# First layer's cross attention (a1) and the gated stage behind it (p2) put into one block

## The reference

```python
x = _attn(_ln(x, g1, b1), _ln(x, g1, b1), Wq1, Wk1, Wv1, Wo1, bo1) + x
x = _attn(_ln(x, g2, b2), context, Wq2, Wk2, Wv2, Wo2, bo2) + x      # 16 heads of 64; scores, softmax, values
x = _geglu_ff(_ln(x, g3, b3), Wp, bp, Wf, bf) + x                    # a * gelu(gate) @ Wf; Wp is 256 x 2048, Wf 1024 x 256
# second layer: 16 heads of 16; self attention, gelu feed-forward, cross attention, gelu feed-forward
```

## Time and profile before

| | |
|---|---|
| median of 3 runs | 3474.93 us (3468.88 to 3476.86) |
| the profiled execution | 3473.62 us, span 3471.8 us |
| PE busy | 3212.7 us, 93% of the span |
| DVE, ACT, POOL busy | 2257.0, 1823.9, 1085.5 us |
| mean granted clock of PE | 0.952 |
| a1 on PE | 966.9 to 1999.4 us |
| p2 on PE | 2016.9 to about 2290 us |

### The profile page before, as it was taken

The page is one execution under the profiler, slowest core; times in us unless marked ns, Lnnn a source line. Parts: engine busy times, 40 slices in busy tenths (PEclk is TensorE's granted clock), DMA queues, the critical chain, the costliest instruction groups (busy, mean ns, idle before and its releaser), DMA issues. The chain is left out here.

```text
span 3471.8 us, 48148 instructions
## 1 busy us (share of the span) xinstructions
PE 3212.7 (93%) x17084; PEld 1842.8 (53%) x17084; DVE 2257.0 (65%) x4098; ACT 1823.9 (53%) x3369; POOL 1085.5 (31%) x537
## 2 busy tenths in 40 slices
PE   7969996999979999999999959979999699999989
PEld 5734443788744444444444447743477544444347
DVE  5447774444356666766666435569866499999844
ACT  4424444444424444444444424448766268888864
POOL 1036663000047777787777800002200000000000
PEclk9979998999979999999999979979999789999999
DMA  6888874999885666666766153154554723333140
GB/s 231 306 202 225 216 210 175 369 334 346 288 185 136 142 153 156 145 141 146 160 147 142 50 192 138 46 181 129 171 197 151 269 67 108 92 99 111 58 137 31
DMA packets 367126, 588.79 MB, mean 170 GB/s; under 512 B 47152, under 2 KB 197216, under 8 KB 365736
## 3 DMA queue, kind: packets, MB, share of 16 engines
q1 hardware_dynamic: 361710, 582.41, 56.8%
q10 hardware_dynamic: 5178, 3.31, 0.4%
HBM read 344.19 MB, written 241.29 MB: 169 GB/s over the span
## 5 line engine op out<-in xcount | busy, mean ns | idle before, releaser
L2164 ACT ACTIVATE a_prob<-a_ring 128x512 f32<-128x512 f32 (+1 forms) x1088 | 575.3, 602 | 665.7 <-PE a_ring L2069 588.9
L2190 DVE TENSOR_REDUCE a_blk_max<-a_ring 128x1 f32<-128x402 f32 x1024 | 519.4, 567 | 325.6 <-PE a_ring L2053 325.5
L1733 ACT ACTIVATE a_prob<-a_ring 128x512 f32<-128x512 f32 (+1 forms) x1088 | 582.2, 605 | 137.1 <-PE a_ring L1657 132.2
L2019 POOL TENSOR_TENSOR a_prob_sum<-a_prob,a_prob_sum 128x1024 f32<-128x1024 f32 x256 | 599.3, 2376 | 2.8 <-ACT a_prob L2164 2.8
L2091 PE MATMUL a_pv<-a_prob,a_v 128*64 128x512 f32 (+1 forms) x2176 | 537.6, 613 | 0.0
L1778 DVE TENSOR_REDUCE a_blk_max<-a_ring 128x1 f32<-128x402 f32 x1024 | 506.8, 566 | 34.6 <-PE a_ring L1644 27.7
L2068 PE MATMUL a_ring<-a_q_stack,a_k_stack 128*128 128x512 f32 (+1 forms) x1088 | 464.6, 427 | 13.4 <-DMA a_q_second<-maxima 13.4
L2069 PE MATMUL a_ring<-a_q_second,a_k_second 65*128 65x512 f32 (+1 forms) x1088 | 435.6, 400 | 0.0
L2019 POOL TENSOR_TENSOR a_prob_sum<-a_prob 128x1024 f32<-128x1024 f32 x128 | 302.0, 2370 | 423.4 <-DVE a_chunk_sum L2221 236.6
L1675 PE MATMUL a_pv<-a_prob,a_v 128*32 128x256 f32 (+2 forms) x4096 | 341.2, 406 | 13.6 <-ACT a_prob L1733 7.8
L1644 PE MATMUL a_ring<-a_k_stack,a_q_stack 63*128 63x402 f32 (+1 forms) x1280 | 282.5, 424 | 39.4 <-DMA a_q_stack<-q_lo_self 18.6
(11 more groups left out here) (268 smaller groups left out, 4676.1 us busy)
## 6 DMA issues: line engine op xcount, KB each, us to landing
a_k_stack<-k_hi_cross SPq DMA_DIRECT2D x96, 400.5 KB, 4.6
a_v<-v_cross SPq DMA_DIRECT2D x48, 768.0 KB
a_k_stack<-k_lo_cross SPq DMA_DIRECT2D x80, 400.5 KB, 6.0
a_k_second<-k_hi_cross SPq DMA_DIRECT2D x32, 801.0 KB, 12.6
v_cross<-p_v_sb SPq DMA_DIRECT2D x48, 512.0 KB
k_hi_cross<-p_split_hi SPq DMA_DIRECT2D x120, 200.0 KB, 3.6
k_lo_cross<-p_split_lo SPq DMA_DIRECT2D x120, 200.0 KB, 4.6
a_q_stack<-q_hi_self SPq DMA_DIRECT2D x64, 256.0 KB, 4.1
```

The lines of the kernel that those rows point to most:

```text
L1733: nc.scalar.activation(prob[0:keys, tau % RC, m, :], ring[0:keys, score_place(e) % BANKS, :], ACT.Exp, scale=a.scale).then_inc(exp_done, 1)
L2019: nc.gpsimd.tensor_tensor(prob_sum[:, h], prob_of(i * NCP + cp, h), other, ALU.add)\
L2164: nc.scalar.activation(prob_of(w, h)[0:keys, ch % 2, :], ring[0:keys, score_bank(e), :], ACT.Exp, scale=a.scale).then_inc(exp_done, 1)
L2190: nc.vector.reduce_max(dst, ring[:, max_bank(g), 0:a.blk], AX.X).then_inc(item_read, 1)
```

## The change

a1 and p2 share one block (`attend_then_feed`, with `attend_wide` taking the block and an `Ahead` of p2's functions).
- Wp's four raw pieces are loaded into the tile of its own low half right behind the loads of a1's group 1 (`load_early`), and rounded and subtracted in steps 7 to 10 of a1, one a step.
- When groups 0 to 30 are done, SP loads x, Wo2's pieces, batch 0's attention output, Wf, sq and sk (`load_first`). ACT rounds Wo2 ahead of step T-2, DVE subtracts ahead of the last group's sums. When all 32 groups are done, SP loads batch 1's output into the tiles of u (`load_second`).
- The last group's denominators (`last_sums`) are made inside batch 0's "after", ahead of its last two of eight pairs of heads. The banks that a1's tail still uses are guarded by `banks_read`.
- p2's steps: batch 1's "after" moves from behind gate 3 to ahead of "scale", its "residual" ahead of gate 0.
- The tiles of p2 have fixed places (`WP_AT`), those of a1 are laid out slot by slot, the slot of group 31 last.

```diff
+WP_AT = {W0_ + "Wo2_hi": 0, W0_ + "Wo2_lo": 8, "o0_hi": 16, "o0_lo": 32, "x_from": 48, "split_hi": 52, "split_lo": 58,
...
-    NO = 2 if before and not attn else 1
+    NO = 2 if before and not cross else 1
     EARLY = 0
     OP = 2
+
+    def o_at(b):
+
+        return b % NO if not geglu else int(before is not None and b == 1)
+
+    def o_loads(b):
+
+        return sum(1 for e in range(1, b + 1) if o_at(e) == o_at(b))
+
+    def o_next(b):
+
+        return [e for e in range(b + 1, B) if o_at(e) == o_at(b)][:1]
 
     def sem(what):
         return pr.sem(f"{name}_{what}")
...
                 steps += window_cross(b)
         elif attn:
-            steps += norm(0, 0, "mean") + split(w_o, w_1) + norm(0, 0, "var") + split(w_1, w_last)
-            steps += norm(0, 0, "scale") + norm(0, 0, "shift") + gates(0, 0, 4) + front(1) + gates(0, 4, 5)
+            steps += norm(0, 0, "mean") + norm(0, 0, "var") + [("piece", i, 0) for i in range(EARLY, len(pieces))]
+            steps += front(1)[:2] + norm(0, 0, "scale") + norm(0, 0, "shift") + front(1)[2:] + gates(0, 0, 5)
             steps += norm(0, 1, "mean") + gates(0, 5, 7) + norm(0, 1, "var") + gates(0, 7, FT) + of(0, outs[:1])
             steps += norm(0, 1, "scale") + of(0, outs[1:2]) + norm(0, 1, "shift") + of(0, outs[2:])
             for b in range(B):
...
@@ -956,13 +1001,15 @@
             sp.dma_start(raw_piece(i), pieces[i][0]).then_inc(w_raw[i % NR], 16)
 
         def load_early(sp):
-            for i in range(EARLY):
+            for i in early:
                 load_piece(sp, i)
             if cross:
                 sp.dma_start(ctx_raw[:], pr.ins["ctx"][0]).then_inc(ctx_loaded, 16)
 
         def load_first(sp):
             sp.dma_start(x_from[:], x_in[0]).then_inc(x_loaded, 16)
+            for i in late:
+                load_piece(sp, i)
             for n, loaded in enumerate(o_first):
                 for h in range(2):
                     sp.dma_start(words(o[0][h][:, n * OP:(n + 1) * OP]), pr.o[after[0].name][h][n * OP:(n + 1) * OP]
@@ -970,13 +1017,16 @@
             for i in range(EARLY, len(pieces)):
                 if raw_after[i] is None:
                     load_piece(sp, i)
-            for b in range(1, NO):
-                load_o(sp, b)
+            if NO > 1 and not geglu:
+                load_o(sp, 1)
+
+        def load_second(sp):
+            load_o(sp, 1)
 
         def load_o(sp, b):
             for h in range(2):
-                sp.dma_start(words(o[b % NO][h][:]), pr.o[after[0].name][h][b * ko:(b + 1) * ko]
-                             .rearrange("g p n -> p g n")).then_inc(o_loaded[b % NO], 16)
+                sp.dma_start(words(o[o_at(b)][h][:]), pr.o[after[0].name][h][b * ko:(b + 1) * ko]
+                             .rearrange("g p n -> p g n")).then_inc(o_loaded[o_at(b)], 16)
 
         def round_piece(act, m):
             act.wait_ge(w_raw[m % NR], 16 * (m // NR + 1))
...
-                        for stored in end.stored_by((b + NO + 1) * ko):
-                            sp.wait_ge(*stored)
-                    sp.wait_ge(d_tile, d_no[step] + 1)
-                    load_o(sp, b + NO)
+                elif kind == "after" and m == 1:
+                    for e in o_next(b):
+                        if end:
+                            for stored in end.stored_by((e + 1) * ko):
+                                sp.wait_ge(*stored)
+                        sp.wait_ge(d_tile, d_no[step] + 1)
+                        load_o(sp, e)
                 elif kind == "residual" and b < LAST:
                     sp.wait_ge(x_summed, KT * (b + 1))
...
                     pe.wait_ge(a_read, a_no[step] - NA + 1)
-                elif end and a_no[step] == NA - 1:
-                    pe.wait_ge(*end.out_copied)
+                elif end and a_no[step] in end.banks_read:
+                    pe.wait_ge(*end.banks_read[a_no[step]])
                 return a_bank(step)
 
             def statistic(out, src):
@@ -1155,6 +1208,8 @@
                     if end:
                         pe.wait_ge(*end.maxima_read)
                     for kt in range(ko):
+                        if end and end.last_sums and kt == ko - 2:
+                            end.last_sums(pe)
                         if kt % OP == 0:
                             pe.wait_ge(o_first[kt // OP], 32)
                         for t in range(KT):
@@ -1166,8 +1221,8 @@
                                 last.then_inc(d_tile, 1)
                 elif kind == "after":
                     if m == 0:
-                        pe.wait_ge(o_loaded[b % NO], 32 * ((b + NO - 1) // NO))
-                    product3(free_d(step), wo, (slice(m * P, (m + 1) * P),), o[b % NO], (slice(None),), ko)\
+                        pe.wait_ge(o_loaded[o_at(b)], 32 * o_loads(b))
+                    product3(free_d(step), wo, (slice(m * P, (m + 1) * P),), o[o_at(b)], (slice(None),), ko)\
                         .then_inc(d_tile, 1)
                 elif kind == "mean":
...
+        for s in (n % SLOTS for n in range(NG - SLOTS, NG)):
+            kst[s], qst[s] = sb(f"k_stack{s}", [P, 2, KP], F32R), sb(f"q_stack{s}", [P, 2, NQ], F32R)
+            k2[s], q2[s] = sb(f"k_second{s}", [65, 2, KP], F32R), sb(f"q_second{s}", [65, 2, NQ], F32R)
+            v[s] = sb(f"v{s}", [P, NC, P])
...
@@ -1977,11 +2042,28 @@
             load_maxima(0)
             load_second(1)
             load_v(1)
+            if ahead:
+                ahead.load_early(sp)
             for n in range(2, SLOTS - 1):
                 load_kq(n)
                 load_second(n)
                 load_v(n)
+            def groups_done(n):
+
+                sp.wait_ge(st_done, n * E)
+                sp.wait_ge(pv_done, n * NC)
+
             for i in range(NG + 3):
+                if ahead and i == NG - 1:
+                    groups_done(NG - 1)
+                    for stored in stored_by(a.groups_b):
+                        sp.wait_ge(*stored)
+                    ahead.load_first(sp)
+                elif ahead and i == NG:
+                    groups_done(NG)
+                    for stored in stored_by(2 * a.groups_b):
+                        sp.wait_ge(*stored)
+                    ahead.load_second(sp)
                 if a.cross:
                     at(load_kq, i + SLOTS - 1)
                     at(load_second, i + SLOTS - 1)
@@ -1994,8 +2076,9 @@
                     at(load_second, i + SLOTS - 1)
                     at(load_v, i + SLOTS - 1)
                     at(store, i - 3)
-            for s in range(OS):
-                sp.wait_ge(o_stored[s], 32 * len(range(s, NG, OS)))
+            if not ahead:
+                for stored in stored_by(NG):
+                    sp.wait_ge(*stored)
 
         @block.gpsimd
         def _(pool):
@@ -2031,6 +2114,15 @@
                     add(i, m)
                     if not dve_sums:
                         merge(i, m)
+
+        def denominators(pe, i):
+            pe.wait_ge(merged, 2 * (i + 1))
+            if i:
+                pe.wait_ge(o_lo_done, i)
+            for h in range(2):
+                last = nc.tensor.matmul(sums[64 * h:64 * h + 64, :], pr.ones[:, 0:64],
+                                        chunk_sum[:, i % CS, h, :], start=True, stop=True)
+            last.then_inc(den_done, 1)
 
         @block.tensor
         def _(pe):
...
@@ -2094,7 +2177,7 @@
 
             def sums_at(w):
                 if w >= DEN_AT and (w - DEN_AT) % NCP == 0 and (w - DEN_AT) // NCP < NG:
-                    denominators((w - DEN_AT) // NCP)
+                    denominators(pe, (w - DEN_AT) // NCP)
 
             maxima(0, pairs_by(-1))
             for w in range(T):
@@ -2107,8 +2190,9 @@
                 sums_at(w)
                 maxima(cut(w), pairs_by(w))
             values(T - 1)
-            for w in range(T, T + DEN_AT):
-                sums_at(w)
+            if not ahead:
+                for w in range(T, T + DEN_AT):
+                    sums_at(w)
 
         @block.scalar
         def _(act):
...
                 if cp == 1 and i:
                     raw_copy(i - 1)
+                if ahead and w - NCP in ahead.early:
+                    ahead.round_piece(act, w - NCP)
+                elif ahead and w == T - 2:
+                    for m in ahead.late:
+                        ahead.round_piece(act, m)
                 if not a.cross and cp == NCP - 1 and i + 1 < NG:
...
             for half in range(2 * (T + HIGH_AT + 1)):
                 w = half // 2
+                if ahead and half % 2 and w - NCP in ahead.early:
+                    ahead.rest_of_piece(dve, w - NCP)
+                elif ahead and half == 2 * T - 1:
+                    for m in ahead.late:
+                        ahead.rest_of_piece(dve, m)
                 if half % 2 == 0:
...
+    return End((item_read, 2 * NG * PAIRS), {2: (o_lo_done, NG), 3: (pv_copied, NG)}, stored_by, lambda pe: denominators(pe, NG - 1))
+
 
 def build(nc, ins, out):
```

(7 more changed lines are left out.)

123 lines of the change are left out of this document (71 added, 52 removed).

## The result

| | before | after |
|---|---|---|
| median | 3471.9 us (3468.35 to 3476.86, 4 runs) | 3435.98 us (3431.46 to 3437.93, 4 runs) |
| ratio, 95% interval | | 0.9893 [0.9882, 0.9905] |
| profiled execution, its span | 3473.62, 3471.8 us | 3434.35, 3432.5 us |

Two later comparisons of the same kernel gave 0.9911 [0.9898, 0.9923] and 0.9900 [0.9883, 0.9916]. The three lie around 0.990, 34 us. The forecast was 3438 us.

The account below looks back on a forecast made before the run. PE was taken to bound a1 and most of p2, with a hole at their boundary. A gain of 37.7 us up to batch 1's mean, less 2 at a1's start, gave 35.7: 3438 us (own range 3433 to 3443).

Parts of the forecast that it names:

- What bounds the kernel: PE bounds a1 and most of p2; from last values to batch 1's mean, 35.4 us of matmuls take 89.
- a sign of being wrong: At the a1 to p2 boundary: batch 1's mean not coming 51 us behind a1's last values (89 originally).
- The end of a1: At a1's end: PE starts batch 0's product 2.4 us late, and residual starts at 2007.5, 22.6 us earlier.
- take turns: In a1's last group: DVE's Wo2 subtractions alternate with POOL's adds, making PE's start and POOL's sums 2.4 us later.
- From residual to the gates: In p2: z is ready 20.3 us after residual starts, at 2027.8, as batch 1's product ends.
- The parts: Split of 37.7 us: 22.6 boundary, 2.5 Wp's pieces leaving the chain, 10.9 batch 1's hidden product, 1.8 warm gates.
- The start of a1: In a1's steps 7 to 10: Wp's early pieces cost 2 us, with no wait for group 2's keys.
- The sum: Whole kernel: 37.7 - 2 = 35.7 us gained, giving 3438 us.
- No blocking: Rival at a1's end: DVE and POOL do not block each other; 41.9 us gained, 3432 us; chance 0.15.
- Start stalls: Rival at a1's start: late keys and maxima, slow PE, dearer early pieces; 12 us lost, 3448 us; chance 0.2.
- New wait in p2: Rival in p2: batch 1's output or x not landed when wanted; 8 us lost, 3446 us; chance 0.05.
- worse streaming: Rival in a1: matmuls stream worse from new SBUF places; at 12 ns more each, 3492 us; chance 0.02.

Follow-up runs that it names:

- yield6: Changed kernel with one wait added: in the last group POOL's seventh add of ten waits for VectorE's two Wo2 subtractions; 3428.2 us, ratio 0.9882.
- yield8: Changed kernel with POOL's pause for VectorE's two Wo2 subtractions ahead of its ninth add in the last group; 3427.18 us in one run.
- pool_halves: Changed kernel with POOL's last eight adds of the last group cut into sixteen halves, still without a pause; 3440.39 us in one run.
- wp_late: Changed kernel with Wp's pieces still loaded early but rounded and subtracted in p2, behind the variance; 3444.67 us, ratio 0.9933.
- gates_first: Changed kernel with batch 1's output product put back behind two gate steps of batch 0; 3449.48 us, ratio 0.9941.
- sums_first: Changed kernel with the last group's denominators ahead of the whole output product instead of ahead of its last quarter; 3434.66 us, ratio 0.9899.
- lo_last: Changed kernel with batch 0's product reordered: matmuls with Wo2's high part first, then the low part, denominators amid the latter; 3433.8 us, ratio 0.9888.
- dve_tail: Changed kernel with VectorE making POOL's last four adds of the last group, denominators behind 24 matmuls; 3427.05 us (0.9878), repeated 3427.88 us (0.9872).

## Why the prediction was right, and where not

**What bounds the kernel: right.** The hole between the last values and batch 1's mean was where the time went, and where it came back from: 32.2 us of a difference of some 34. The prediction named a sign of being wrong, a mean that does not come 51 us behind the last values. It came at 56.55, so by its own sign the account of this stretch was wrong by 5 us, in the step that follows.

**The end of a1: the mechanism half right, its price wrong.** The prediction had DVE and POOL exclude each other, which they do, but "take turns" here. In the last group DVE never got one: yield6, yield8 and pool_halves show that it waits until POOL's run of adds ends. The forecast had PE waiting 2.4 us and POOL's sums 2.4 us late; it was 6.8 and 0. From values to residual that gave 22.5 us instead of 2007.5 - 1990.07 = 17.4, a miss of 5.1 us. So the end of a1 gave 39.98 - 22.5 = 17.5 us, counted from the values to the residual, where the forecast had 22.6. Of the 5.1, 4.4 are the longer wait. The rest is the product's slow clock, which was foreseen, but at 1.8 us: its 36 matmuls took 10.75 us (1992.12 to 2002.87), against 8.2 + 1.8.

The prediction took turns from the earlier trace rows and did not read them to the end. It calls them the one place where a subtraction of two SBUF tiles meets POOL. There are two in a row, and POOL's two operations stand back to back:
```profile
2497.16 1.48 POOL L1619 TENSOR_TENSOR a_o_lo<-a_o_full,a_o_hi 128x512 fp32r<-128x512 f32 x1 [6.33 <-ACT a_o_hi L1717]
2498.60 1.46 POOL L1614 TENSOR_TENSOR a_o_full<-a_o_full,a_inv 128x512 f32<-128x512 f32 x1
```
```profile
2498.95 1.39 DVE L989 TENSOR_TENSOR p_L_xattn_ck_w_hi<-p_w_raw,p_L_xattn_ck_w_hi 64x256 fp32r<-64x256 f32 x1
```
The first subtraction ended at 2497.41 + 1.50 = 2498.91, well ahead of the end of POOL's second operation at 2500.06, so VectorE did get in between the two. The second subtraction was held until that operation's end (2500.34). Turns were a fair reading of this place. What failed is carrying them over to a run of eight equal adds.

"SBUF — State Buffer" of the Trainium skill, section "Who interferes with whom", has the shared pair of SBUF ports held by the one who issues first for one whole instruction. The trace agrees that the two engines exclude each other. On an owner that has its next instruction ready the section says nothing; here POOL kept VectorE out over at least three ends of its own instructions in after and seven in pool_halves. So the engines of this kernel meet not only at semaphores: these two met without one.

**That DVE and POOL can take turns** is also in the traces after, in a1's second group. The fourth early piece came at 1037.47 in after, in the second of POOL's adds:
```profile
1037.47 2.09 DVE L1042 TENSOR_TENSOR p_L_xattn_Wp_lo<-p_w_raw,p_L_xattn_Wp_hi 128x1024 fp32r<-128x1024 f32 x1
```
```profile
1032.91 5.57 POOL L2102 TENSOR_TENSOR a_prob_sum<-a_prob 128x1024 f32<-128x1024 f32 x2 [12.95 <-DVE a_chunk_sum L2310]
1038.44 19.73 POOL L2102 TENSOR_TENSOR a_prob_sum<-a_prob,a_prob_sum 128x1024 f32<-128x1024 f32 x8
```
It ended at 1039.56, 1.1 us behind the end of that add, and POOL's next eight took 19.73 us instead of 18.72 (before, and wp_late, in the same group): here DVE came in between two adds. The same shows in all eleven executions that have the early pieces (2.05 to 2.10 us, and 19.7 to 19.8 for the eight adds). That place is the change from the group's first two adds, with two inputs from `prob`, to the eight that add to `prob_sum`; in the last group only ends between adds of the same form passed. At the end of a2, in all fourteen executions, VectorE got in between a subtraction and a multiplication. So wherever it got in, POOL's next instruction was of another kind than the last, and wherever it was held over an instruction's end, of the same. Whether that decides, or how POOL's waits stand there, no run tests. It stays open.

**From residual to the gates: right.** Forecast 20.3 us from residual to z and the end of batch 1's product at the same moment; it was 2028.18 - 2007.82 = 20.4 us, with 0.2 us of waiting. Residual to mean was 34.05 us, forecast 33.9.

**The parts.** The order was priced at 10.9 + 1.8 and gates_first gave 12.4. Wp's pieces were priced at 2.5 for leaving their old place, and that is what the rows show (2.4 us from residual to variance). Behind the variance they cost 4.5 and, with the clock, 7.1: the price of an instruction on VectorE depends on whether VectorE waits there anyway. Wp's pieces back in the old place, beside the new order, were not run. The denominators inside the product were worth nothing that sums_first can tell; in the prediction this had no term of its own.

**The start of a1: too dear.** Forecast 2 us. The stretch takes 1022.6 to 1023.6 us in the three executions without Wp's work in it (mean 1023.1) and 1022.7 to 1024.0 in the eleven with it (mean 1023.6), so some 0.5 us, less than the scatter. There is no wait for the keys of group 2. The exclusion costs POOL about 0.9 + 1.0 us in one group (5.57 for two adds against 4.71 in the earlier trace rows, and the eight above), and PE does not wait for it.

**The sum.** Forecast 37.7 - 2 = 35.7; measured 32.2 at the boundary and nothing at the start. The two errors, 5.1 lost at the end of a1 and 2 not lost at the start, cancel in part. That the first comparison's 3435.98 lies so close to 3438 is in part the scatter of stages that were not touched.

**The rivals.** No blocking: out; the residual came 22.5 us behind the values, not 13.2. In yield6, where POOL's pause takes the blocking away at the price of 2.4 us on the sums, it came at 14.8. Start stalls: the queue did form, the cost did not. Behind Wp's loads the row of maxima of group 1 is loaded 1016.22 - 1010.34 = 5.9 us behind its store in after, against 1017.44 - 1015.37 = 2.1 before, and PE waits for neither. New wait in p2, worse streaming: none seen; a1's length is the same within 1 us.

## What to carry to other kernels

A VectorE instruction with two SBUF inputs, put beside a GpSimd that has a backlog of SBUF adds, should be priced at the whole backlog and not at one instruction. If it is on the path, a pause in GpSimd's queue that waits for it, or moving the end of the backlog to VectorE, costs little (yield6: 2.36 us of POOL's time) and gave back 9 to 12 us at this place. That is shown for a run of equal adds; between unlike GpSimd instructions VectorE got in here. The four early pieces' 4.6 us on VectorE cost 2.4 us where it would have waited in part anyway, and all of it a few instructions on, so price work at its place in the chain. Set executions side by side by stage, between marks on the bound engine, before a difference of a few microseconds is explained: the stretch in question repeated within 0.03 to 1.2 us, the start of a1 only within 11.

## What the runs showed of the hardware that I had not expected

- VectorE's wait for GpSimd's run: 10.4 us with no pause, 5.8 with a pause 4.7 us later than yield6's, 1.2 with that one; over 16 half instructions 11.5 us.
- A VectorE subtraction with one input in PSUM is not held: `a_o_lo` took 0.69 us at 1979.94 in after, in the middle of POOL's run.
- PE's variance, after the same wait of 2.17 us, took 1.98 us in yield6 and sums_first and 2.9 to 3.8 in lo_last and yield8. The kernel alone doesn't decide it: dve_tail took 3.13 us, with granted clocks of 0.73 and 0.50 in two stretches of 1.5 us from its start, dve_tail_again 1.98 us at 1.00, with the same waits ahead. That is the 1.2 us between those two, and it may be most of the 2 us between yield6 and lo_last, whose residuals are 0.5 us apart the other way.
